# Streaming the first MLP projection's weight halves tile by tile in a decoder kernel on one Trainium2 core

## The reference

```python
h = shift_token(x)
mu = h.mean(-1, keepdims=True)
var = h.var(-1, keepdims=True)
h = (h - mu) / jnp.sqrt(var + 1e-05) * lg + lb
h = h @ w1 + b1                      # w1: 256 x 1364
a, g = jnp.split(h, 2, axis=-1)      # 682 hidden features each
h = a * jax.nn.gelu(g, approximate=False)
x = x + h @ w2 + b2
```

## Time and profile before

| | |
|---|---|
| device time, median of 3 runs | 1173.26 us (1170.98 to 1173.38) |
| profiled execution, its own time | 1168.97 us |
| its span | 1167.2 us |
| mean granted TensorE clock | 0.997 |
| PE busy | 1130.6 us (97%) |
| DVE, ACT, POOL busy | 72%, 60%, 53% |
| DMA queue of SP | 22.0% of 16 DMA engines' span |

### The profile page before, as it was taken

The page is one execution under the profiler, slowest core; times in us unless marked ns, Lnnn a source line. Parts: engine busy times, 40 slices in busy tenths (PEclk is TensorE's granted clock), DMA queues, the critical chain, the costliest instruction groups (busy, mean ns, idle before and its releaser), DMA issues.

```text
span 1167.2 us, 20315 instructions
## 1 busy us (share of the span) xinstructions
PE 1130.6 (97%) x6858; PEld 895.0 (77%) x6858; DVE 837.8 (72%) x2481; ACT 705.8 (60%) x1742; POOL 612.8 (53%) x641
## 2 busy tenths in 40 slices
PE   8899999999999999999989999999999999999987
PEld 6778787888787877676667787887878878777676
DVE  6788787878788655769886767768666677684553
ACT  3578777778776513453566756546656476575822
POOL 1455657565655311229886546547456465573420
PEclk9899999999999999999999999999999999999999
DMA  8124545554532501021021000300002100001011
GB/s 270 37 56 132 172 125 170 148 172 125 164 113 73 181 19 55 1 95 37 19 113 62 1 1 1 127 1 2 1 20 97 55 1 1 1 7 67 1 38 35
DMA packets 40549, 81.48 MB, mean 70 GB/s; under 512 B 5888, under 2 KB 18304, under 8 KB 39936
## 3 DMA queue, kind: packets, MB, share of 16 engines
q1 hardware_dynamic: 40448, 80.20, 22.0%
HBM read 41.04 MB, written 22.36 MB: 54 GB/s over the span
## 4 chain that ended last, share of the span: by engine, by line
PE 86%; DVE 6%; ACT 5%; issue 2%; POOL 1%; DMA 0%; SPq 0%; DVEq 0%; ACTq 0%; POOLq 0%
PE psum L1551 52%; PE psum L1649 6%; PE psum L1631 5%; PE psum L1781 5%; PE psum L1830 5%; PE psum L1797 4%; PE psum L1815 4%; PE psum L1763 2%; ACT probs L909 1%; DVE probs L1156 1%; ACT lp L993 1%; PE psum L1558 1%; PE psum L1737 1%; PE psum L1854 1%; PE psum L1843 1%
## 5 line engine op out<-in xcount | busy, mean ns | idle before, releaser
L751 POOL TENSOR_TENSOR probs<-probs,rden 128x128 f32<-128x128 f32 (+3 forms) x256 | 178.3, 728 | 80.8 <-DVE rden L1168 80.8
L993 ACT ACTIVATE lp<-lp,lneg,rn 128x256 f32<-128x256 f32 (+1 forms) x256 | 143.6, 568 | 17.3 <-DVE lneg L1385 17.2
L909 ACT ACTIVATE probs<-probs,negmax 128x128 f32<-128x128 f32 (+3 forms) x256 | 140.8, 552 | 11.5 <-DVE negmax L1163 10.9
L1156 DVE CUSTOM_DVE_ANT_0 probs<-psum,causal 128x512 f32<-128x512 f32 (+3 forms) x256 | 109.9, 485 | 16.2 <-PE psum L1551 16.0
L784 POOL TENSOR_TENSOR lp<-lp,lrden 128x128 f32<-128x128 f32 x64 | 25.6, 400 | 176.0 <-DVE lrden L1390 176.0
L796 POOL TENSOR_TENSOR rn<-ssm,neg_half 128x8 f32<-128x8 f32 x64 | 108.1, 1690 | 0.0
L1373 DVE CUSTOM_DVE_ANT_0 lp<-psum,local 128x256 f32<-128x256 f32 (+1 forms) x256 | 84.2, 385 | 20.6 <-PE psum L1781 20.6
L787 POOL TENSOR_TENSOR lp<-lp,lrden 128x768 f32<-128x768 f32 x64 | 93.9, 1467 | 0.0
L980 ACT ACTIVATE sq<-psum 128x512 f32<-128x512 f32 x64 | 37.8, 594 | 86.8 <-PE psum L1551 82.1
L874 ACT ACTIVATE pT<-psum 128x512 f32<-128x512 f32 (+1 forms) x96 | 46.9, 517 | 67.9 <-PE psum L1631 67.8
L1631 PE MATMUL psum<-ident,probs 128*128 128x128 f32 x640 | 86.1, 274 | 1.2 <-POOL probs L751 1.2
(11 more groups left out here) (172 smaller groups left out, 3244.7 us busy)
## 6 DMA issues: line engine op xcount, KB each, us to landing
k<-k_round SPq DMA_DIRECT2D x128, 128.0 KB, 2.4
w_raw<-in_w_all SPq DMA_DIRECT2D x22, 380.0 KB, 3.9
w_scratch<-w_half SPq DMA_DIRECT2D x22, 380.0 KB, 4.3
w_scratch<-w_rest SPq DMA_DIRECT2D x22, 380.0 KB, 4.6
x<-in_x SPq DMA_DIRECT2D x8, 512.0 KB, 6.0
aw<-in_w_quads SPq DMA_DIRECT2D x4, 768.0 KB, 5.3
wqkv_lo<-w_scratch SPq DMA_DIRECT2D x6, 512.0 KB, 6.5
wqkv_hi<-w_scratch SPq DMA_DIRECT2D x6, 512.0 KB, 4.5
```

The costliest lines, as they stand in the source:

```text
L751: ins = pool.tensor_tensor(pr, pr, rden[:, u % 2, h, i:i + 1].broadcast_to([P, TRI[i]]), ALU.mult)
L909: ins = act.activation(pr, pr, ACT.Exp, bias=negmax[:, u % 2, h, i:i + 1], scale=ADH ** -0.5, accum_out=den[:, u % 2, h, i:i + 1])
L993: ins = act.activation(pr, pr, ACT.Exp, bias=lneg[:, u % 2, h, w:w + 1], scale=rn[:, m % 2, w, 0, 2 * j + h:2 * j + h + 1], accum_out=lden ...
L1156: ins = dve.tensor_tensor_reduce(probs[:, u % 2, h, TRI_AT[i]:TRI_AT[i + 1]], bank[:, at:at + TRI[i]], causal[:, S - TRI[i]:S], 1.0, -3e38 ...
```

## The change

`w1_hi` and `w1_lo` shrink from a whole layer to two slots (`W1_RING`) of one tile each. Tile number n = 6 m + f goes to slot n % 2. In every step, when the value half of tile f has ended, SP loads the tile two places further on (`next_w1`), in two transfers, high and low (`load_w1`): 248 columns in each of two rows of a partition, so runs of 992 bytes, 248 KB a transfer and 496 KB a tile (244 columns for tile 4; 128 for tile 5, 128 KB a transfer). TensorE waits for each tile's pair (`w1_tile` says on which semaphore and to which count). In step 7 the tiles 2, 3 and 4 (`W1_END`) come from a third place, `w1_end`, which lies where `wqkv_lo` stood, and are loaded when tile 0 of step 6 has ended; tile 5 of step 7 is loaded into slot 1 after tile 1 of step 7. Since SP now has work in each step, its program walks through TensorE's order, and the transfers that stood there (`wqkv`, `tab`, `wo`, `w2`, `x2`) stand at their places in that walk. What is computed is the same.

```diff
-        w1_lo = sbt(ctx, "w1_lo", [P, E2, 2 * HID], F32R)
-        w1_hi = sbt(ctx, "w1_hi", [P, E2, 2 * HID], F32R)
+        w1_lo = sbt(ctx, "w1_lo", [P, W1_RING, E2, 2 * FROWS[0]], F32R)
+        w1_hi = sbt(ctx, "w1_hi", [P, W1_RING, E2, 2 * FROWS[0]], F32R)
...
+        def w1_tile(m, f):
+
+            if m == STEPS - 1 and f in W1_END:
+                i = W1_END.index(f)
+                return w1_end[:, 0, i], w1_end[:, 1, i], ld_w1_end, 2 * 16 * (i + 1)
+            n = NF * m + f
+            turn = n // W1_RING - (f > W1_END[-1] and m == STEPS - 1)
+            return w1_hi[:, n % W1_RING], w1_lo[:, n % W1_RING], ld_w1[n % W1_RING], 2 * 16 * (turn + 1)
...
+            def load_w1(m, f):
+                hi, lo, done, _ = w1_tile(m, f)
+                cols = slice(2 * FAT[f], 2 * FAT[f + 1])
+                for half, tile in enumerate((hi, lo)):
+                    src = w_dram[m // B, half, :, W_AT[3]:W_AT[4]].rearrange("p (e c) -> p e c", e=E2)
+                    sp.dma_start(tile[:, :, 0:2 * FROWS[f]].bitcast(F32), src[:, :, cols]).then_inc(done, 16)
+
+            def next_w1(m, f):
+                wait_full(sp, plan["w1a", m, f])
+                m, f = divmod(NF * m + f + W1_RING, NF) if m < STEPS - 1 else (m, NF - 1)
+                load_w1(m, f)
...
+            for what, *at in pe_order:
+                if what == "w1":
+                    m, f = at
+                    if m < STEPS - 1 or f == 1:
+                        next_w1(m, f)
+                    if at == [B - 1, NF - 1]:
+                        for tp in range(2):
+                            wait_read(sp, plan["wo", B - 1, tp])
+                        layer_wo(1)
...
+                if what == "w1" and at == [STEPS - 2, 0]:
+                    for f in W1_END:
+                        load_w1(STEPS - 1, f)
+                if what == "qkv" and at[0] == B - 1 and at[1] == T - 1:
+                    c = "qkv".index(at[2])
+                    wait_full(sp, plan[at[2], B - 1, T - 1])
+                    layer_wqkv_lo(1, c)
+                    layer_wqkv_hi(1, c)
+                if what == "Tqk" and at == [B - 1, T - 1]:
+                    wait_read(sp, plan["q", B - 1, T - 1])
+                    wait_read(sp, plan["k", B - 1, T - 1])
+                    layer_tab(1)
...
             def hidden_part(m, f):
+                w_hi, w_lo, loaded, n = w1_tile(m, f)
+                pe.wait_ge(loaded, n)
                 if f == 0:
                     pe.wait_ge(hn_lo, E2 * (m + 1))
-                    if m % B == 0:
-                        pe.wait_ge(ld_w1, 2 * 16 * (m // B + 1))
```

More of the change, by code:

```diff
@@ L52 @@
 GELU_T = 2
+W1_RING = 2
+W1_END = (2, 3, 4)
 RUN_FIRST = 24
@@ L127, in build @@
         raw.close()
+        raw = ExitStack()
+        w1_end = sbt(raw, "w1_end", [P, 2, len(W1_END), E2, 2 * FROWS[0]], F32R)
+        raw.close()
         wqkv_lo = sbt(ctx, "wqkv_lo", [P, 3, E2, INNER], F32R)
@@ L266, in build @@
         x2_st = sem("x2_st")
-        ld_rot, ld_small, ld_lwo, ld_w1, ld_w2 = (
-            sem(n) for n in ("ld_rot", "ld_small", "ld_lwo", "ld_w1", "ld_w2"))
+        ld_rot, ld_small, ld_lwo, ld_w2 = (
+            sem(n) for n in ("ld_rot", "ld_small", "ld_lwo", "ld_w2"))
+        ld_w1 = [sem(f"ld_w1_{i}") for i in range(W1_RING)]
+        ld_w1_end = sem("ld_w1_end")
         ld_wqkv = [sem(f"ld_w{what}") for what in "qkv"]
@@ L597, in layer_wqkv_hi @@
                     .then_inc(ld_wqkv[c], 16)
-            def layer_w1(l):
-                sp.dma_start(flat(w1_hi[:, :, :]).bitcast(F32), w_dram[l, 0, :, W_AT[3]:W_AT[4]]).then_inc(ld_w1, 16)
-                sp.dma_start(flat(w1_lo[:, :, :]).bitcast(F32), w_dram[l, 1, :, W_AT[3]:W_AT[4]]).then_inc(ld_w1, 16)
+            def load_w1(m, f):
[8 more added lines that the diff above has]
+                load_w1(m, f)
             def layer_w2(l):
@@ L686, in _ @@
             layer_wo(0)
-            layer_w1(0)
+            for f in range(W1_RING):
+                load_w1(0, f)
             layer_w2(0)
@@ L693, in _ @@
             sp.dma_start(shift[:, :, :], a["c_shift"]).then_inc(ld_shift, 16)
[L695 to L718, removed]
+            for what, *at in pe_order:
[7 more added lines that the diff above has]
+                        layer_wo(1)
+                if what == "w1" and at == [STEPS - 3, NF - 1]:
+                    wait_full(sp, plan["v", STEPS - 1, T - 1])
+                    sp.wait_ge(l_ssm, 2 * T * STEPS)
+                    for b in range(B):
+                        sp.dma_start(x2[:, b, :, :], x2_dram[b].rearrange("(t p) e -> p t e", p=P)).then_inc(x2_ld[b], 16)
+                if what == "w1" and at == [STEPS - 2, 0]:
[10 more added lines that the diff above has]
+                    layer_tab(1)
+                if what == "w2" and at == [B - 1, 1]:
+                    for tp in range(2):
+                        wait_full(sp, plan["w2", B - 1, tp])
+                    layer_w2(1)
@@ L1857, in hidden_part @@
             def hidden_part(m, f):
+                w_hi, w_lo, loaded, n = w1_tile(m, f)
+                pe.wait_ge(loaded, n)
                 if f == 0:
                     pe.wait_ge(hn_lo, E2 * (m + 1))
-                    if m % B == 0:
-                        pe.wait_ge(ld_w1, 2 * 16 * (m // B + 1))
                 for what in ("w1g", "w1a") if f < NF - 1 else ("w1g",):
                     rows = FROWS[f] if f < NF - 1 else P
-                    lo = 2 * FAT[f] + (rows if what == "w1a" else 0)
+                    lo = rows if what == "w1a" else 0
                     use = plan[what, m, f]
@@ L1867, in hidden_part @@
                     product(bank[0:rows, :], [(w[:, e, lo:lo + rows], h[:, e, :]) for e in range(E2)
-                                              for w, h in ((w1_hi, hnT_lo), (w1_lo, hnT_hi), (w1_hi, hnT_hi))])\
+                                              for w, h in ((w_hi, hnT_lo), (w_lo, hnT_hi), (w_hi, hnT_hi))])\
                         .then_inc(full[use[0]], 1)
```

## The result

| | before | after |
|---|---|---|
| device time, median | 1171.85 us (1170.59 to 1173.38, 8 runs) | 1178.51 us (1175.17 to 1182.52, 8 runs) |
| profiled execution, its own time | 1168.97 us | 1178.59 us |
| its span | 1167.2 us | 1176.8 us |
| mean granted TensorE clock | 0.997 | 0.994 |

The changed kernel is slower: ratio 1.0059, 95% interval 1.0045 to 1.0073, some 6.7 us. The forecast was 1176.8 us, 1.0030 of the median that it started from. So the sign came true and the time is inside the range, but the loss is nearly twice the 3.5 us of the sum. That the time lies so near is in part luck: the median that the forecast started from, 1173.26 us, was 1.4 us above the one of this comparison. Where the rest of the loss comes from is the question of this study.

The account below looks back on a forecast made before the run. TensorE, busy 97% of the span, was taken as the bound. Profiled 1168.97 us + 0 (waits) + 0 (traffic) + 3.5 (tile 6.3) = 1172.5, or 1176.8 us against the median 4.3 us higher; range 1173.6 to 1180.4.

Parts of the forecast that it names:

- the sum: Whole kernel: profiled 1168.97 us + 0 + 0 + 3.5 = 1172.5 us, against the median 1176.8 us, 0.3% slower.
- (1): TensorE, all steps: 48 extra waits on instructions that already wait for a bank cost 0.
- (2): DMA, whole kernel: `w1` loaded 8 times instead of 2, some 17 MB more, costs 0.
- (3): Middle steps' tile loads: a pair lands in 3.75 us, the tightest gap is 4.9 us, so they cost nothing.
- the line: Landing time of loads with 1 KB runs, from the `x2` loads: 2.2 us + 3.13 us per 1,000 KB.
- D: Middle steps: tiles late there too, at tiles 5 and 2, 6 us more, 1183 us; chance 0.07.
- (4): Step 6: tile 6.3, queued behind 6.2 and the `w1_end` transfers, starts 3.5 us late; 6.2 is 0.2 us late.
- (5): From tile 6.3 to the end: no pause absorbs the delay, so all 3.5 us go to the end.
- A: Tile 6.3: its delay as worked out, 2.4 to 4.3 us, 1175.7 to 1177.6 us; chance 0.45.
- B: Behind tile 6.3: the pause also throttles TensorE's clock, 3.5 + 3.4 us, 1180.2 us; chance 0.18.
- C: Tile 6.3: only SP's issue counts, delay 1.4 up to 2.3 us, 1174.7 to 1175.6 us; chance 0.24.
- E: Whole kernel: no delay or a gain, 1173 us or less; chance 0.06.

Follow-up runs that it names:

- e10: The change with three slots, no `w1_end`, and a filler tile restoring the old SBUF addresses: 1172.44 us against 1172.72 for before, ratio 0.9994.
- e13: e7 again with nothing altered (three slots, no `w1_end`): 1174.59 us against 1172.97 for before, ratio 1.0005.
- e12: The change plus unused SBUF, so that everything behind `w1_hi` keeps its old addresses: 1178.06 us against 1172.97 for before, ratio 1.0041.
- e5: The change plus 16 unused matmuls on TensorE ahead of tile 6.3's wait: 1177.64 us against 1172.34 for before, ratio 1.0047.
- e4: The change with `w1_end` loaded at the same place in two transfers instead of six: 1180.3 us against 1172.34 for before, ratio 1.0071.
- e1: The change with the six `w1_end` transfers issued when tile 6.3 has ended: 1174.3 us against 1172.34 for before, ratio 1.0017.
- e2: The change with the six `w1_end` transfers behind 6.3's pair and ahead of 6.4's: 1174.6 us against 1171.76 for before, ratio 1.0022.
- e3: As e1, with six 8 KB transfers at the old place of the `w1_end` loads: 1175.48 us against 1172.34 for before, ratio 1.0021.
- e7: The change with three slots and no `w1_end`, tiles loaded three places ahead: 1174.43 us against 1171.76 for before, ratio 1.0016.

## Why the prediction was right, and where its sizes were off

**(1) and (2), the waits and the traffic, 0: right.** Middle steps are as long as before, within 0.01 us, with 48 more waits and 16.8 MB more. e10 and e13, which have all of the traffic and all of the waits, are within 0.1% of before. A cost of under 1 us isn't excluded by that: at the granted clock of 0.994 e10 is 0.3 us under before and e13 0.8 us over it, each in its own comparison.

**(3), tiles of the middle steps in time: right but for 0.23 us.** A pair lands 3.0 us after its second issue and 3.4 us after its first (1098.35 to 1101.75), where the line gave 3.75. Tile 5 keeps its margin, and D falls. Tile 1.5, with `wqkv` ahead of it, was due to have 1.3 us to spare and was 0.23 us late. The working had left out that a packet of instructions can take its turn on a DMA engine: in the 0.8 us from 735.0 one takes 16.1% of 16 engines, 2.06 us' worth of one. Two steps of the tile's semaphore were late there: all but the last two of the semaphore's steps have come by 739.79, and those two come at 740.77 and 741.10. That the packet made them late is argued from the coincidence, not tested at this place. `tab` was issued at 747.72 and landed at 753.2, later than the 751 of the working but in time: VectorE's first use of it stands at 757.10, 2.0 us later than before, as everything else at that place does.

**(4), tile 6.3, 3.5 us late: right in mechanism, mis-sized by 0.6 us.** All steps of it can be read in the trace: SP issues the pair of 6.2 at once and then the six, it is free 4.0 us after the first issue (predicted 4.0), and 6.3 stands behind. The term that was off is the train: 9.9 us by the line of `x2`, 10.6 us measured, and tile 6.3 had to wait 4.05. The 0.2 us at 6.2 did not occur, since 6.2 landed at 1101.75, 0.2 us ahead of its start. Of the 10.6 us, the last 0.63 us is a single step's: 31 of the 32 had come after 10.0 us. e12 and e5 have the same picture (0.68 and 0.65 us), and in each a packet of queue 8 falls into the train (at 1104.86 in after). Still, the packet isn't shown to be the cause. In the kernel before, the last step of the fourth load of `x2`, on which the line rests, also comes 0.50 us behind the one ahead of it, with no such packet near. And the wait doesn't need it: in e4 the last step comes only 0.13 us behind the 31st, and the tile waits 3.85 us. The pair of 6.4, issued at 1105.00 onto the same full engines, isn't seen to draw it out: the transfers kept their distance of about 0.75 us up to the end of 6.3, and 6.4's steps came behind 6.3's. Why the train took 10.6 us and not 9.9 stays open beyond this. The Trainium skill's fit ("DMA: Bandwidth & Descriptors", section "Anatomy of one DMA"), which was taken on another issuing path, gives the estimate of 7.8 us for the train; the 10.6 us of the trace are far from it, though for a single pair, by the fit an estimate of 3.2 us, it is near the 3.4 measured.

**(5), all of the delay goes to the end: right.** At the same granted clock of 0.994 the kernel is 5.0 us slower, and e12 at 0.994 is 1177.33 (2 runs) against 1172.76 (9 runs) of before in its own comparison, 4.6 us. The wait is 4.05 of that; the clock's part is not in these numbers, since runs of equal clock are compared. In the same way e1 is 1.6 us over before at 0.996 and e2 1.9 us at 0.994, with waits of 1.53 and 1.70 us.

**A or B.** I gave them as alternatives, and they are one case. The delay is A's (2.4 to 4.3 us); but the clock did fall behind it, in all three profiles with a wait of about 4 us (after, e4, e12), and not behind 1.53, 1.84 and 1.70 us in e1, e3 and e2. The step that failed is that the sum has no term for the clock: it stood only in B, at a chance of 0.18, as if A's delay could come without it. The cost is 1.3 to 1.6 us (e5; tile 6.3), not the 3.4 of B, since the low stretch here lasted 3.4 us and not 6.8. The Trainium skill ("TensorE: Matmul & The Clock Gate", section "Why this matters for your kernels") warns of idle gaps in the middle of a kernel; three profiles of three agree for the 4 us gap.

**The sum, as measured.** 4.05 (6.3) + 0.23 (1.5) + 1.3 to 1.6 (clock behind 6.3) = 5.6 to 5.9 us of the 6.7. The interval of the ratio, 5.3 to 8.6 us, holds it. What may be left, up to 1 us, is within the chance of the clock in other places: I can't attribute it.

**C, the train is only an issue delay:** falls by e4 (issue in time, 3.85 us of wait). **E:** falls by the measurement.

## What to carry to other kernels

A load that is placed early "because there is room" is not free when one queue serves everything: whatever is issued behind it waits for its bytes. So reckon the landing of the next urgent transfer with all that stands ahead of it in the queue, and leave a margin, since the last of a load's 32 steps came 0.6 us behind the others here, and 1.7 us in e1. If a stall of some microseconds on TensorE can't be avoided, count the slow clock behind it as well. And compare small effects over the stretch of the profile that they touch, because the chance of the clock elsewhere (here some 4 us between two executions of one kernel) is larger than they are.

## What the runs showed that I had not expected

Transfers of the kind "instruction" show up in the trace as queue 8, 56 packets of 16 KB in the execution of after, beside a queue 14 with smaller ones. One packet of queue 8 takes 0.9 to 2.1 us. In e1, the 248 KB load that met one landed after 4.7 us instead of 3.0, with one step of its semaphore late. Where the packets fall isn't fixed: in e7 and e13, one kernel, they stand 3.8 us apart against tile 6.0. So a tile with little margin may be late in one execution and in time in another; no run here shows that for one kernel.

Longer runs did not help: 1,480 KB in two transfers with runs of 2,960 bytes took as long as in six with runs of 992 bytes. The engines were full in both (364 GB/s in after and 377 GB/s in e4 between 1106 and 1108), so between these two forms neither the number of transfers nor the length of the runs was the limit.
